# Order of the last group's second norm, gate and shared products, and GpSimd's ids in four steps

## The chip, the cores and the metric

One core of one Trainium2 chip. The time is device microseconds of one execution of the program. The engines are TensorE (PE), VectorE (DVE), ScalarE (ACT), GpSimd (POOL) and SyncE (SP); each works through its own instructions in their written order and waits on semaphores.

## The reference

A transformer layer on 16 images with 193 tokens each (a class token, 64 patches, 128 text tokens), 128 features wide:

```
h = concat(class, patches @ W + b) * pos;  h = concat(h, txt)
h = h + attention(layernorm(h))          # 8 heads, linear attention with elu + 1, rotary, a 3-tap convolution
x = layernorm(h)                         # the second norm
shared = (silu(x @ sw1) * (x @ sw3)) @ sw2
scores = x @ gate_w.T                    # 8 experts
idx = top_k(scores + biases, 2);  p = sigmoid(top_k(scores, 2)); p = p / sum(p)
h = h + shared + sum over the two experts e of a token:
        p_e * ((silu(x @ w1[e]) * (x @ w3[e])) @ w2[e])
```

## The kernel before

All is one core's work in three stages.

*Attention loop.* Two images make a group, so there are G = 8 groups of three 128-row tiles; the 16 class rows are one more tile (CLS), which goes with the last group. While group i is in the attention, the groups in front of it go through the second norm, the gate and the choice of experts. `choices(g)` (VectorE) finds both experts of each token, `place(g)` (TensorE) counts with matmuls how many tokens of an expert come before, `places(g)` and `positions(g)` (VectorE) make each token's row in the buffer `xs_dram`, and GpSimd scatters the normed rows there, two scatters a tile (L861). Each scattered row carries an id (where the result goes) and a share (its p). For groups 0 to 5 GpSimd makes both itself: `goals(g)` the ids, `shares(g)` the shares from ScalarE's exponentials (`odds`).

*Handover.* After the loop the last two groups finish these steps, while TensorE works through the shared products: for each chunk c of 384 tokens, `shared_up(c, m)` for m = 0, 1 (L1572, L1575, into two banks), `shared_silu(c, m)` (ScalarE, L675), `shared_mul(c, m)` (VectorE, L1159), `shared_down(c)` (TensorE, L1587), `shared_add(c)` (VectorE, L1165). A `shared_up` waits until the `shared_mul` two before it has read its bank. Chunks 0 to 5 and chunk 6's `shared_up` come ahead of the experts. ScalarE also rounds the eight experts' weights (`round_w13`, L614) and VectorE keeps what the rounding lost (`remainder_w13`, L1174). For the last group the chain is: second statistics and norm (`x2_done`), `turn_second` (L1477), ScalarE's copy of the turned rows (`x2T`, L723), `gate` (L1484), a copy of the scores, `choices`, `place`, `places`, `positions`, and GpSimd's last eight scatters. `turn_second(g)` also waits for `places(g - 1)`, which reads the same bank. ScalarE changes its function table between exp/ln and Silu (L695, L702, L713).

*Expert loop.* 56 tiles of 128 rows. SyncE loads them once all scatters have landed and the table of tiles is done; TensorE turns each (L1658), VectorE splits it (L1298, L1300), TensorE multiplies (L1669), and so on. Chunks 7 and 8 of the shared products follow behind.

The order on each engine is that of the code. Nothing else sets it.

## Time and profile before

| what | us |
|---|---|
| median of 3 runs | 250.85 (250.84 to 251.06) |
| the profiled execution's own time | 250.12 |
| its span, first to last instruction | 248.3 |
| TensorE busy | 221.4 (89%) |
| VectorE busy | 186.1 (75%) |
| ScalarE busy | 159.4 (64%) |
| GpSimd busy | 134.4 (54%) |

The attention loop ends at about 104 us, and the expert loop begins at about 147 us. A busy share is a mean over the stages; what ends a stage is read from the chain of waits and from the timeline of each engine. In a timeline a row is one instruction, or several of one kind that follow each other (x3), with the time when the first starts and the time until the last one's result; the next instruction of the engine can start a little before that.

### The profile page before, as it was taken

Reading aid. Unit: us, or ns where it says so; the run is one execution under the profiler, and the core shown is the slowest. Engines: PE = TensorE matmul, PEld = TensorE weight load, DVE = VectorE, ACT = ScalarE, POOL = GpSimd, SP = SyncE. Lnnn points to the kernel's source line nnn. Section 1 sums busy time; section 2 is a strip of 40 time slices with the busy share of each in tenths; the row PEclk is TensorE's granted clock in tenths of the full one; section 3 lists DMA queues with packets and bytes.
Section 4 is the critical chain, followed back from the end, with each engine's and each line's share of the span. In section 5 each row is a group of like instructions: output and inputs, shape, how many; then the busy total and the mean of one; then the engine's idle time right before and its main releaser. Section 6 shows DMA issues by size and latency. Waiting matters only on the chain.

```text
span 248.3 us, 5612 instructions
## 1 busy us (share of the span) xinstructions
PE 221.4 (89%) x1485; PEld 189.5 (76%) x1485; DVE 186.1 (75%) x706; ACT 159.4 (64%) x435; POOL 134.4 (54%) x178
## 2 busy tenths in 40 slices
PE   3898889999999999888989979999999999999930
PEld 2878778889898989756676658888888888887720
DVE  3548899998998989988977777666666666665760
ACT  3055676768687878869843266777777767776630
POOL 1400001258787778878777704666666666666500
PEclk9999999999999999999999999999999999999995
DMA  6999973142425101010113231423333333348657
GB/s 210 354 350 356 325 274 125 27 189 65 187 67 206 44 25 43 11 56 11 55 54 115 62 83 43 115 68 101 88 88 83 93 94 85 86 128 235 185 137 192
DMA packets 31566, 31.75 MB, mean 128 GB/s; under 512 B 4338, under 2 KB 27419, under 8 KB 30768
## 3 DMA queue, kind: packets, MB, share of 16 engines
q1 hardware_dynamic: 27240, 24.60, 32.7%
q0 software_dynamic: 3392, 6.38, 7.9%
q10 hardware_dynamic: 904, 0.41, 0.6%
q8 instruction: 13, 0.21, 0.4%
q14 instruction: 17, 0.14, 0.2%
HBM read 22.83 MB, written 9.06 MB: 128 GB/s over the span
## 4 chain that ended last, share of the span: by engine, by line
PE 57%; DVE 19%; issue 7%; ACT 6%; POOL 4%; DMA 4%; SPq 1%; DVEq 0%; POOLq 0%; ACTq 0%
PE bank L1669 15%; PE bank L1689 10%; PE bank L1678 5%; PE bank L1381 5%; POOL xs_dram L861 4%; DVE att L956 3%; DVE att L949 3%; DVE st L890 3%; PE bank L1658 3%; PE bank L1464 2%; PE bank L1450 2%; PE bank L1484 2%; DMA xp_both<-in_patches 2%; DVE hrow L998 2%; PE bank L1587 2%
## 5 line engine op out<-in xcount | busy, mean ns | idle before, releaser
L872 POOL DMA_INDIRECT y_dram<-att,goal x56 | 55.8, 996 | 35.8 <-ACT att L766 35.2
L861 POOL DMA_INDIRECT xs_dram<-xd,pos_i x50 | 52.2, 1044 | 21.8 <-issue 18.9
L1381 PE MATMUL bank<-wt,xp_both 128*128 128x128 f32 x288 | 40.7, 296 | 5.0 <-DMA xp_both<-in_patches 5.0
L1381 PEld LDWEIGHTS bank<-wt,xp_both 128*128 128x128 f32 x288 | 38.5, 208 | 6.3 <-DMA xp_both<-in_patches 5.3
L1689 PE MATMUL bank<-w_sb,att 128*128 x224 | 34.5, 277 | 0.0
L1298 DVE CAST xsT_h<-bank 128x128 fp32r<-128x128 f32 x56 | 16.3, 292 | 24.0 <-PE bank L1658 22.5
L752 ACT ACTIVATE att<-bank 128x256 f32<-128x256 f32 x56 | 21.5, 384 | 19.1 <-PE bank L1669 19.1
L1689 PEld LDWEIGHTS bank<-w_sb,att 128*128 128x128 f32 x224 | 29.4, 191 | 0.3 <-issue 0.2
L1669 PE MATMUL bank<-xp_both,xsT_h 128*128 x56 | 26.8, 479 | 0.0
L1311 DVE TENSOR_TENSOR att<-att,bank 128x256 f32<-128x256 f32 x56 | 23.2, 414 | 1.6 <-ACT att L752 1.6
L766 ACT ACTIVATE att<-bank,goal 128x128 f32<-128x128 f32 x56 | 20.6, 368 | 4.6 <-PE bank L1689 0.5
L1669 PE MATMUL bank<-xp_both,xsT_l 128*128 x56 | 22.1, 394 | 0.0
L1669 PE MATMUL bank<-w,xsT_h 128*128 x56 | 21.9, 392 | 0.0
L1678 PE MATMUL bank<-cst,att 128*128 128x128 f32 x112 | 21.5, 274 | 0.4 <-DVE att L1311 0.4
L759 ACT COPY att<-bank 128x256 f32<-128x256 f32 x56 | 20.9, 372 | 0.8 <-PE bank L1678 0.7
L1678 PEld LDWEIGHTS bank<-cst,att 128*128 128x128 f32 x112 | 13.8, 140 | 5.8 <-DVE att L1311 1.4
L1300 DVE TENSOR_TENSOR xsT_l<-bank,xsT_h 128x128 fp32r<-128x128 f32 x56 | 16.3, 292 | 1.9
L675 ACT ACTIVATE sh_s<-bank 128x384 f32<-128x384 f32 (+1 forms) x18 | 8.0, 456 | 13.3 <-PE bank L1575 12.4
L1658 PE MATMUL bank<-cst,xs_all 128*128 128x128 f32 x56 | 15.3, 273 | 1.4 <-DMA xs_all<-xs_dram 1.4
L1307 DVE COPY goal<-xs_all 128x2 f32<-128x2 f32 x56 | 14.9, 267 | 0.0
L1587 PEld LDWEIGHTS bank<-sw_sb,sh_h 128*128 128x128 f32 (+1 forms) x88 | 10.4, 187 | 5.2 <-DVE hrow L1165 2.2
L1572 PE MATMUL bank<-x2T,sw 128*128 128x384 f32 (+1 forms) x36 | 13.9, 467 | 0.4 <-DVE sh_h L1159 0.4
(225 smaller groups left out, 512.2 us busy)
## 6 DMA issues: line engine op xcount, KB each, us to landing
xp_both<-in_patches SPq DMA_DIRECT2D x6, 1152.0 KB
xs_all<-xs_dram SPq DMA_DIRECT2D x56, 65.0 KB, 1.9
xd<-y_dram SPq DMA_DIRECT2D x8, 384.0 KB, 5.1
w<-in_w SPq DMA_DIRECT2D x2, 1024.0 KB, 10.4
y_dram<-att,goal POOLq DMA_INDIRECT x56, 2.3
xs_dram<-xd,pos_i POOLq DMA_INDIRECT x50
xp_both<-in_patches SPq DMA_DIRECT2D x1, 768.0 KB, 5.4
hrow<-in_txt SPq DMA_DIRECT2D x2, 384.0 KB, 7.3
```

Of the source, the lines that this page charges most:

```text
L752: A(hs[q][:], bank[2 + q][:, 0:HID], ACT.Silu).then_inc(silu_done[at], 1)
L759: nc.scalar.copy(hmT[q][:], bank[4 + q][:, 0:HID].rearrange("p (m t) -> p m t", m=2)).then_inc(hmT_done[at], 1)
L766: A(ys[buf][:], bank[6 + q][:, 0:D], ACT.Copy, scale=goal[buf][:, 1:2]).then_inc(ys_done[at], 1)
L861: nc.gpsimd.indirect_dma_start(out=xs_dram[:, :], out_offset=bass.IndirectOffsetOnAxis(ap=pos_i[0:rows, j, k:k + 1], axis=0), in_=xd[0:row ...
L872: nc.gpsimd.indirect_dma_start(out=y_dram[:, :], out_offset=bass.IndirectOffsetOnAxis(ap=goal[u][:, 0:1].bitcast(I32), axis=0), in_=ys[u][ ...
L1298: V.tensor_copy(xsT_h[q][:], bank[q][:, 0:P]).then_inc(xh_done, 1)
L1311: V.tensor_tensor(hm[q][:], hs[q][:], bank[2 + q][:, HID:2 * HID], ALU.mult).then_inc(hm_done[at], 1)
L1381: M(ps[:, 0:D], xp[p][:, k, :], wt[:, k, :], start=(k == 0), stop=False)
L1658: T(bank[q][:, 0:P], xs[u][:, 0:D], ident).then_inc(tx_done[slot(u, 0)], 1)
L1669: last = M(bank[2 + q][:, 0:2 * HID], x[q][:], w[:, bass.ds(first * 2, 2 * HID)], start=(i == 0), stop=(i == 2))
L1678: last = T(bank[4 + q][:, P * m:P * m + P], hm[q][:, P * m:P * m + P], ident)
L1689: last = M(bank[6 + q][:, 0:D], hmT[q][:, m, :], w[:, bass.ds(first + m * D, D)], start=(m == 0), stop=(m == 1))
```

## The change

Four parts:

1. On VectorE, ScalarE and TensorE the last group's second norm, its rows and its gate stand ahead of shared products, and some weight remainders behind. 2. `s_col` and `scores(G - 2)` stand ahead of the Silu table on ScalarE. 3. GpSimd's `goals` makes both ids with one subtraction of six elements, one comparison and one addition (four instructions in place of five), from a second table in `dest_sb` that holds the bare row numbers. 4. The power in `shares` becomes a VectorE `RECIPROCAL` in `positions(g)`, g below 6: VectorE waits there for GpSimd's sum, GpSimd for the reciprocal.

```diff
-WEIGHED = 7
+WEIGHED = 6
+SUMMED = 5
...
@@ ScalarE, behind columns2(G - 2)
+            act.wait_ge(s_done, G)
+            nc.scalar.copy(s_col[:].rearrange("p (g b) -> p g b", b=2), s_all[:, :, 0:2]).then_inc(s_done, 1)
+            scores(G - 2)
             act.preload_act_table(ACT.Silu)
             shared_silu(0, 0)
-            scores(G - 2)
-            act.wait_ge(s_done, G)
-            nc.scalar.copy(s_col[:].rearrange("p (g b) -> p g b", b=2), s_all[:, :, 0:2]).then_inc(s_done, 1)
             shared_silu(0, 1)
-            round_w13(3)
             act.preload_act_table_set("natural_log_exp_and_others")
...
             act.preload_act_table(ACT.Silu)
             shared_silu(1, 0)
-            shared_silu(1, 1)
-            shared_silu(2, 0)
-            round_w13(4)
             act.wait_ge(nm2_done, G)
             A(xd[:, CLS - 1, 0, 0:D], hrow[:, CLS - 1, :], ACT.Identity, bias=nm2[:, CLS - 1:CLS],
               scale=rs2[:, CLS - 1:CLS]).then_inc(x2_done, 1)
+            shared_silu(1, 1)
+            shared_silu(2, 0)
+            round_w13(3)
             shared_silu(2, 1)
             act.wait_ge(x2_turned, G)
...
-            round_w13(5)
             act.wait_ge(gate_done, G)
...
+            round_w13(4)
+            shared_silu(3, 0)
+            round_w13(5)
+            shared_silu(3, 1)
             round_w13(6)
-            shared_silu(3, 0)
-            shared_silu(3, 1)
...
@@ GpSimd
-                then_pool(nc.gpsimd.tensor_tensor(crossed[:], chosen[:, :, 0], chosen[:, :, 1], ALU.subtract))
+                then_pool(nc.gpsimd.tensor_tensor(crossed[:], chosen[:], chosen[:, :, ::-1], ALU.subtract))
                 then_pool(nc.gpsimd.tensor_scalar(apart[:], crossed[:], 0.0, float(NID), ALU.is_gt, ALU.mult))
-                nc.gpsimd.tensor_tensor(xd[:, at, 0, D].bitcast(I32), ids[:, at, 0], apart[:], ALU.add)
-                nc.gpsimd.tensor_tensor(xd[:, at, 1, D].bitcast(I32), ids[:, at, 1], apart[:], ALU.subtract)
+                nc.gpsimd.tensor_tensor(xd[:, at, :, D].bitcast(I32), ids[:, at, :], apart[:], ALU.add)
...
-                then_pool(nc.gpsimd.tensor_tensor(odds_sum[:], odds_sum[:], minus[:], ALU.pow))
-                then_pool(nc.gpsimd.tensor_tensor(xd[:, at, :, D + 1], odds[:, :, ::-1], odds_sum[:].rearrange(
+                pool.wait_ge(pos_done, 2 * g + 1)
+                then_pool(nc.gpsimd.tensor_tensor(xd[:, at, :, D + 1], odds[:, :, ::-1], odds_part[:].rearrange(
...
-                pool.wait_ge(pos_done, g + 1)
+                pool.wait_ge(pos_done, g + 1 + min(g + 1, EARLIER))
@@ VectorE, positions(g)
+                if g < EARLIER:
+                    dve.wait_ge(pool_chain, WEIGHED * g + SUMMED)
+                    V.reciprocal(odds_part[:], odds_sum[:]).then_inc(pos_done, 1)
                 dve.wait_ge(pr_done, g + 1)
@@ VectorE, the handover (without its waits and its unchanged lines)
-            remainder_w13(0)
             places(G - 3)
             positions(G - 3)
+            remainder_w13(0)
...
-            remainder_w13(2)
             second_rows(G - 1)
-            shared_mul(0, 0)
             second_stats(G - 1)
...
-            shared_mul(0, 1)
+            shared_mul(0, 0)
...
+            shared_mul(0, 1)
             choices(G - 2)
-            shared_add(0)
-            shared_mul(1, 0)
...
-            shared_mul(1, 1)
-            places(G - 2)
-            positions(G - 2)
...
-            remainder_w13(3)
+            places(G - 2)
+            positions(G - 2)
+            shared_mul(1, 0)
+            shared_add(0)
+            shared_mul(1, 1)
+            remainder_w13(2)
+            choices(G - 1)
             shared_mul(2, 0)
-            shared_mul(2, 1)
-            remainder_w13(4)
-            shared_add(1)
-            choices(G - 1)
             places(G - 1)
             positions(G - 1)
...
+            shared_add(1)
+            shared_mul(2, 1)
+            remainder_w13(3)
+            shared_mul(3, 0)
             shared_add(2)
-            shared_mul(3, 0)
+            remainder_w13(4)
@@ TensorE, behind shared_up(2, 0)
             place(G - 2)
+            turn_second(G - 1)
             shared_up(2, 1)
+            gate(G - 1)
             shared_down(1)
-            turn_second(G - 1)
-            gate(G - 1)
-            shared_down(2)
             shared_up(3, 0)
             place(G - 1)
+            shared_down(2)
             shared_up(3, 1)
```

The instructions as they stand in both kernels, at three places. A line number of the kernel after is one or two off from that of the kernel before. First ScalarE from the copy of group 6's turned rows (`x2T`) on, before:

```order
L478 COPY x2T<-bank6 128x384
L695 ACT_TABLE_LOAD
L675 ACTIVATE sh_s0<-bank5 128x384
L488 COPY sc<-bank6 128x24
L699 COPY s_col<-s_all 128x16
L675 ACTIVATE sh_s1<-bank2 128x384
L614 CAST xp_both<-w13 128x512
L702 ACT_TABLE_LOAD
L707 ACTIVATE lv2<-mv2 128x3
L707 ACTIVATE lv2<-mv2 16x1
```

and after:

```order
L479 COPY x2T<-bank6 128x384
L697 COPY s_col<-s_all 128x16
L489 COPY sc<-bank6 128x24
L699 ACT_TABLE_LOAD
L676 ACTIVATE sh_s0<-bank5 128x384
L676 ACTIVATE sh_s1<-bank2 128x384
L702 ACT_TABLE_LOAD
L707 ACTIVATE lv2<-mv2 128x3
L707 ACTIVATE lv2<-mv2 16x1
```

The sum's class columns (`s_col`) and the scores (`sc`) have moved ahead of the table, and a rounding (L614) is gone from here.

TensorE from `shared_up(2, 1)` of the kernel before on (L1572 and L1575 are a `shared_up`, L1587 a `shared_down`, L1477 `turn_second`, L1484 the gate):

```order
L1572 MATMUL bank<-x2T,sw 128x384
L1575 MATMUL bank<-x2T,sw 128x384
L1587 MATMUL bank<-sw_sb,sh_h 128x128 x6
L1477 MATMUL bank<-cst,xd 128x128 x3
L1477 MATMUL bank<-cst,xd 128x16
L1484 MATMUL bank<-cols,x2T 128x8 x3
L1484 MATMUL bank<-cols,x2T 16x8
L1587 MATMUL bank<-sw_sb,sh_h 128x128 x6
L1572 MATMUL bank<-x2T,sw 128x384
L1575 MATMUL bank<-x2T,sw 128x384
```

and after, from `turn_second` on:

```order
L1479 MATMUL bank<-cst,xd 128x128 x3
L1479 MATMUL bank<-cst,xd 128x16
L1574 MATMUL bank<-x2T,sw 128x384
L1577 MATMUL bank<-x2T,sw 128x384
L1486 MATMUL bank<-cols,x2T 128x8 x3
L1486 MATMUL bank<-cols,x2T 16x8
L1589 MATMUL bank<-sw_sb,sh_h 128x128 x6
L1574 MATMUL bank<-x2T,sw 128x384
L1577 MATMUL bank<-x2T,sw 128x384
```

`turn_second` has moved ahead of `shared_up(2, 1)`, the gate behind it, and only one `shared_down` stands between the gate and `shared_up(3, 0)`. Behind `place(7)`, which ends with the total (L1501, now L1503), TensorE has before:

```order
L1498 MATMUL bank<-bc,ones_b 128x8
L1501 MATMUL bank<-total,ones_b 128x8
L1572 MATMUL bank<-x2T,sw 128x384
L1575 MATMUL bank<-x2T,sw 128x384
L1572 MATMUL bank<-x2T,sw 128x384
```

and after:

```order
L1500 MATMUL bank<-bc,ones_b 128x8
L1503 MATMUL bank<-total,ones_b 128x8
L1589 MATMUL bank<-sw_sb,sh_h 128x128 x6
L1574 MATMUL bank<-x2T,sw 128x384
L1577 MATMUL bank<-x2T,sw 128x384
L1574 MATMUL bank<-x2T,sw 128x384
```

The `shared_down` that stood behind the gate now stands here, ahead of `shared_up(3, 1)`.

VectorE up to the end of the last group's choices (L1034 writes `total`), before:

```order
L1159 TENSOR_TENSOR sh_h0<-sh_s0,bank1 128x384
L1159 TENSOR_TENSOR sh_h1<-sh_s1,bank0 128x384
L1174 TENSOR_TENSOR w13<-w13,xp_both 128x512
L1165 TENSOR_TENSOR hrow<-bank3,hrow 128x384
L1014 TENSOR_TENSOR scb<-sc,gateb_sb 128x32
L1017 MAX mx8<-scb 128x8 x4
L1022 MAX_INDEX ix8<-mx8,scb 128x8 x4
L1024 TENSOR_TENSOR pick<-cst,ix8 128x64
L1029 TENSOR_SCALAR pick<-pick,cst 128x16
L1030 TENSOR_TENSOR bc7<-pick 128x32
L1034 TENSOR_REDUCE total<-bc7 128x8
```

and after, from the end of these choices (L1033) on:

```order
L1029 TENSOR_TENSOR bc7<-pick 128x32
L1033 TENSOR_REDUCE total<-bc7 128x8
L1161 TENSOR_TENSOR sh_h0<-sh_s0,bank1 128x384
L1041 TENSOR_TENSOR prod<-pick,bank6 128x64
L1057 TENSOR_REDUCE pos_2<-prod 128x8
L1058 TENSOR_REDUCE pos_i<-pos_2 128x4
L1059 TENSOR_REDUCE pos_i<-pos_2 128x4
L1230 TENSOR_TENSOR tab_p<-bank6,cst 128x8
L1167 TENSOR_TENSOR hrow<-bank3,hrow 128x384
L1161 TENSOR_TENSOR sh_h1<-sh_s1,bank0 128x384
```

Before, both products of chunk 2 (L1159), a remainder (L1174) and `shared_add(1)` (L1165) stand ahead of the choices. After, the first product stands behind the choices, and the second behind places, positions (L1041 to L1059), `tab_p` and `shared_add(1)`.

## Rows read from the trace of the kernel before

**Rows 1.** Chain of waits, 100 to 150 us; columns: start us, us, what
```profile
123.25 0.65 PE bank L1575 x2
...
141.47 1.94 DMA xs_dram<-xd,pos_i
```

**Rows 2.** Timeline of TensorE, handover; columns: start us, us, instruction, [idle before <-releaser]
```profile
118.97 1.58 PE L1587 MATMUL bank<-sw_sb,sh_h 128*128 128x128 f32 x12
120.39 0.81 PE L1572 MATMUL bank<-x2T,sw 128*128 128x384 f32 x2
...
126.31 0.97 PE L1484 MATMUL bank<-cols,x2T 128*128 128x8 f32 x8 [0.58 <-ACT x2T L723]
...
130.40 0.89 PE L1572 MATMUL bank<-x2T,sw 128*128 128x384 f32 x2
...
146.75 0.49 PE L1669 MATMUL bank<-xp_both,xsT_h 128*128 x1
```

**Rows 3.** Timeline of VectorE, handover
```profile
116.25 0.56 DVE L998 TENSOR_TENSOR hrow<-bank,hrow 128x384 f32<-128x384 f32 x1
...
117.18 0.67 DVE L890 BATCH_NORM_STATS2 st<-hrow 128x6 f32<-128x128 f32 x3
...
118.12 0.25 DVE L1203 TENSOR_TENSOR hrow<-bank,hrow 16x128 f32<-16x128 f32 x1
...
122.81 0.18 DVE L1042 TENSOR_TENSOR prod<-pick,bank 128x48 f32<-128x48 f32 x1
...
123.41 0.84 DVE L1221 TENSOR_SCALAR xd<-hrow,rs,nm 128x128 f32<-128x128 f32 x3
...
127.57 0.19 DVE L1014 TENSOR_TENSOR scb<-sc,gateb_sb 128x32 f32<-128x32 f32 x1
...
129.72 0.22 DVE L1034 TENSOR_REDUCE total<-bc 128x8 bf16<-128x40 bf16 x1
130.58 0.22 DVE L1042 TENSOR_TENSOR prod<-pick,bank 128x64 f32<-128x64 f32 x1 [0.64 <-PE bank L1501]
...
146.24 0.29 DVE L1300 TENSOR_TENSOR xsT_l<-bank,xsT_h 128x128 fp32r<-128x128 f32 x1
```

**Rows 4.** Timeline of VectorE: positions in the attention loop, and a reciprocal
```profile
87.28 0.17 DVE L1052 TENSOR_REDUCE pos_i<-prod 128x6 int32<-128x48 f32 x1
...
99.41 0.17 DVE L1052 TENSOR_REDUCE pos_i<-prod 128x6 int32<-128x48 f32 x1
99.50 0.61 DVE L974 SCALAR_TENSOR_TENSOR hl<-xT,cols,hl 128x384 f32<-128x384 f32 x1
...
152.77 0.19 DVE L1287 RECIPROCAL mx<-mx 128x7 f32<-128x7 f32 x1
```

**Rows 5.** Timeline of TensorE: attend() in the attention loop
```profile
101.55 0.92 PE L1464 MATMUL bank<-qq,ksm 128*128 128x193 f32 x4 [0.24 <-ACT ksm L550]
```

**Rows 6.** Timeline of GpSimd: first scatters, ids and odds
```profile
51.66 1.25 POOL L861 DMA_INDIRECT xs_dram<-xd,pos_i  x1 [5.82 <-issue]
...
59.54 1.01 POOL L834 TENSOR_TENSOR crossed<-chosen 128x3 f32<-128x3 f32 x1
...
62.98 0.20 POOL L844 TENSOR_TENSOR odds_sum<-odds 128x3 f32<-128x3 f32 x1
...
86.75 0.19 POOL L834 TENSOR_TENSOR crossed<-chosen 128x3 f32<-128x3 f32 x1
...
88.60 0.38 POOL L844 TENSOR_TENSOR odds_sum<-odds 128x3 f32<-128x3 f32 x1
...
124.33 1.35 POOL L861 DMA_INDIRECT xs_dram<-xd,pos_i  x1 [0.30 <-issue]
```

**Rows 7.** Timeline of ScalarE, handover
```profile
114.79 1.28 ACT L695 ACT_TABLE_LOAD   x1
116.08 0.49 ACT L675 ACTIVATE sh_s<-bank 128x384 f32<-128x384 f32 x1
...
125.76 0.49 ACT L723 COPY x2T<-bank 128x400 f32<-128x400 f32 x1 [1.33 <-PE bank L1477]
```

More of the change, by code:

```diff
@@ L99, in destinations @@
     ids = flat + np.arange(2)[None, None, :] * NID
-    return np.concatenate([ids.reshape(P, 2 * J), np.full((P, 1), BIG)], 1).astype(np.int32)
+    flat = np.broadcast_to(flat, ids.shape)
+    return np.concatenate([ids.reshape(P, 2 * J), np.full((P, 1), BIG), flat.reshape(P, 2 * J)], 1).astype(np.int32)
 def build(nc, patches, txt, w_tok, cls, pos, wqk, bqk, small, gate_b,
@@ L122, in build @@
         ident, mask = cst[:, C_ID:C_ID + P], cst[:, C_MASK:C_MASK + P]
-        dest_sb = sb("dest_sb", [P, 2 * J + 1], I32)
+        dest_sb = sb("dest_sb", [P, 4 * J + 1], I32)
         wt = sb("wt", [P, KB, D])
@@ L190, in build @@
         pos_2 = sb("pos_2", [P, LATE, 2])
-        apart = sb("apart", [P, 3], I32)
+        apart = sb("apart", [P, 3, 2], I32)
         chosen = sb("chosen", [P, 3, 2])
-        crossed = sb("crossed", [P, 3])
+        crossed = sb("crossed", [P, 3, 2])
         odds = sb("odds", [P, 3, 2])
-        minus = sb("minus", [P, 3])
-        odds_sum = sb("odds_sum", [P, 3])
+        odds_sum, odds_part = sb("odds_sum", [P, 3]), sb("odds_part", [P, 3])
         pos_i = sb("pos_i", [P, J, 2], I32)
@@ L817, in _ @@
             nc.gpsimd.memset(xd[:, FROM:, :, D + 1:D + 2], 1.0).then_inc(ids_ready, 1)
-            nc.gpsimd.memset(minus[:], -1.0).then_inc(ids_ready, 1)
-            pool.wait_ge(ids_ready, 3)
-            ids = dest_sb[:, 0:2 * J].rearrange("p (j k) -> p j k", k=2)
+            pool.wait_ge(ids_ready, 2)
+            ids = dest_sb[:, 2 * J + 1:4 * J + 1].rearrange("p (j k) -> p j k", k=2)
             links = [0]
```

## The prediction

> **What bounds the kernel now.** I read three views in this order. The chain of waits first: up to 100 us it runs round the attention loop, from 147 us to the end round the expert loop on TensorE, and between them it ends in GpSimd's scatters, of which ten follow one another and the last lands at 141.47 + 1.94 = 143.41 [rows 1]. So at first sight the handover is bound by GpSimd. Then TensorE's own rows: in all that time it works through the shared products, and the first expert product starts at 146.75 [rows 2]. Then VectorE's: the last input that it makes for that product is ready at 146.24 + 0.29 = 146.53 [rows 3], only 0.22 us sooner, and in front of it stand the last shared products. So two lines arrive together: scatters, and shared products. Speeding one gives at most 0.22 us; delaying either costs nearly all of the delay, since the expert loop behind is a TensorE chain that gives nothing back.
>
> **The change part by part.** Times below are those of the profiled execution.
>
> *The loop.* positions(g) for g = 0 to 4 gets a RECIPROCAL. Three elements are not in the trace; seven take 0.19 [rows 4]. VectorE starts a small instruction some 0.09 after the last (99.41 to 99.50 [rows 4]), so each costs 0.09, or 0.19 if nothing overlaps. It delays nm1, ScalarE's rows and key sums behind it, and TensorE's attend(), which waits 0.24 for those sums and for nothing else [rows 5]. I find no cover: 5 x 0.09 = 0.45 us, with 0 to 0.95 as ends. positions(5) stands before a VectorE idle and costs nothing.
>
> VectorE now also waits there for GpSimd's odds_sum(g); queued behind it are tap_before, nm1 and heads, and TensorE waits for those. Six scatters and the step before them take 51.66 to 59.54 = 7.9 us; the steps from the subtraction to the odds' sum took 59.54 to 63.18 = 3.6 in group 1 and 86.75 to 88.98 = 2.2 in group 3 [rows 6], now one instruction fewer. Between VectorE's positions and the first scatter I allow 1.1 (group 6's first scatter at 124.33 comes 0.84 after its positions, and the share's product is ahead now [rows 3, 6]). Sum 11.0 to 12.6 against a loop of 99.41 - 87.28 = 12.13 [rows 4]. Mostly it fits; with four such groups (1 to 4) the ends are 0 and 4 x 0.5 = 2. I take 0.2, near the lower end, as the loop is the longer in most of that range.
>
> *GpSimd's four steps.* The id instruction and the power go. GpSimd reaches later groups sooner, but their scatters then wait for VectorE's positions, so nothing of it reaches the handover except through groups 6 and 7 (rivals).
>
> *ScalarE's table.* s_col and scores(6) now stand ahead of the Silu table. Before, the load ran from 114.79, in the idle of others, and the first Silu followed 0.01 behind it at 116.08 [rows 7]. Now ScalarE first waits for the attention's sum (VectorE's second rows start at 116.25, and mixed_rows and the sum come before; I put the sum at 115.6), copies twice, loads from 115.8 to 117.1 and has its first Silu done by 117.6.
>
> The page "ScalarE: Activation LUTs" of the Trainium skill (What ACT_TABLE_LOAD costs) adds a drain of 1380 ns to a load of 1283 ns at every switch of sets. The load agrees with 1.28; the 0.01 behind it [rows 7] shows no drain, and the measurement decides. By the page the first Silu would come 1.38 later, and the sum below would grow by about 1.
>
> *Norm and gate, forward.* The addition of second rows and the product behind it took 0.93 for two (116.25 to 117.18 [rows 3]), so 0.47 a piece and 0.55 to the result. Without a product between, the statistics wait for the addition's result, 116.25 + 0.56 = 116.8; the class row's addition follows 0.94 later (117.18 to 118.12 [rows 3]), at 117.75, and shared_mul(0,0) at 117.95, ready at 118.5. Before it was ready by 117.3, and here the loss starts: shared_up(1,1) takes its bank over and now waits until 118.5, a TensorE idle of 1.1.
>
> From there the chain is TensorE's. A shared_up takes 1.30 (two halves of 0.65 [rows 1], the last result 0.16 later), a shared_down 118.97 to 120.39 = 1.42 [rows 2]. shared_up(1,1) ends at 119.8, shared_down(0) at 121.2, shared_up(2,0) at 122.5, place(6) gives its result at 122.8. The second norm's rows are done long since, at 122.1: ahead of their 123.41 there stood two products, an addition and the 0.60 of places and positions [rows 3], 2.0 us in all. But turn_second(7) waits for places(6) too, and ScalarE's shared_silu(2,0) and TensorE's shared_up(2,1) wait for shared_mul(1,0), which VectorE now has behind positions(6): 122.8 + 0.60 = 123.4, ready at 124.0. shared_up(2,1) gives its result 1.46 later, at 125.45, and shared_silu(2,1) needs it. Behind that Silu, on ScalarE, stands the x2T copy of the last group: it takes 0.49 as before [rows 7], and is done at 126.4. The gate runs 126.4 to 127.4; it ran 126.31 to 127.28 [rows 2]. So the rows come 2 us sooner and the gate no sooner at all.
>
> *Behind the gate.* The scores' copy ends at 127.65. choices(7) takes 129.72 + 0.22 - 127.57 = 2.37 [rows 3] and ends at 130.0, place(7) at 130.4; VectorE's places(7) started at 130.58 before [rows 3], now at 130.45. Here the second and larger loss sits. Before, TensorE went from place(7) straight to shared_up(3,1) at 130.40 [rows 2]. Now shared_down(2) is there, and needs shared_mul(2,1), which VectorE does behind places, positions and tab_p (0.7, from the 0.60 for three tiles), shared_add(1) (0.47) and its own 0.55: ready at 132.2. TensorE idles 1.8 us, spends 1.42 on shared_down(2), and starts shared_up(3,1) at 133.65 in place of 130.40, 3.25 later. Everything behind it is the same in both kernels and in the same order, and was dense on TensorE; the weights' remainders that VectorE has put off fit into its idles there. So the last inputs come at 146.53 + 3.25 = 149.78 and the first expert product at 149.8: 3.05 later than 146.75.
>
> **Sum.** 250.12 + 3.05 + 0.45 + 0.2 = 253.82. The profiled execution lies 0.73 below the median of the runs (250.85), so 254.55 on that scale; I say 254.5.
>
> **Rivals.**
>
> *VectorE and GpSimd in lockstep.* The condition: GpSimd's steps fall beside VectorE's long rotary instructions in every group, not only in group 1. For it: the same subtraction took 1.01 us at 59.54 and 0.19 at 86.75 [rows 6], and since GpSimd is about 2 us sooner in each round, its steps move to where group 1's were. Against it: scatters then run free of them. Price: up to 0.5 more a round, 2 in all: 256.3. The page "SBUF — State Buffer" of the Trainium skill (Who interferes with whom) says that a VectorE instruction with two SBUF inputs holds off a GpSimd instruction that reads SBUF for its whole length. The 1.01 against 0.19 agrees.
>
> *The scatters alone bind (faster).* If the shared products had 3 us to spare, the end would go with GpSimd. positions(6) is ready at 123.5, GpSimd already waits and starts at 123.8, not 124.33 [rows 6]; the last group's positions at 131.2 are in time for a scatter line that ends 0.5 sooner. With the reciprocals hidden under the 0.24 [rows 5]: 250.85 - 0.5 = 250.3; with them on the path, 250.8, no change. It decides only if VectorE's first expert input comes by 146.6, which asks for shared_mul(2,1) 3 us sooner than I have it. The 0.22 of [rows 2, 3] speaks against it. The same case would be a gate that really comes forward: if ScalarE got to the x2T copy right behind turn_second(7), at 123.7, the gate would be at 125.4.
>
> *A part of the loss only.* The gate 1 us sooner than I put it and no loop cost: 250.85 + 2.0 = 252.9.
>
> **How the numbers follow.** A measurement of this kernel can tell about 0.2% (0.5 us) from no change. Forecast, 253.3 to 255.5: 0.68. Lockstep, 255.5 to 257.5: 0.12. Part of the loss, 251.4 to 253.3: 0.09. No change: 0.05. Faster: 0.06. So slower 0.89, same 0.05, faster 0.06. The range from 252.5 to 256.1 leaves out the two last cases and the outer halves of the others.
>
> **What would show it.** Right: TensorE idle of about 1 us ahead of the shared_up behind the class row, and of 1.8 ahead of the shared_down behind place(7), "released by VectorE's product"; the gate within 0.3 of 126.3 plus the loop's shift; GpSimd's last scatter long done when the first expert product starts; the expert loop and the tail unchanged in length. In the loop, RECIPROCAL rows below 0.2, and none of them with a wait on GpSimd longer than 0.3. Wrong: an x2T copy that starts at once behind turn_second(7), no idle behind place(7), or the chain of waits still in the scatters at 143 us.

## The result, and the profile after

| what | before | after |
|---|---|---|
| median in one comparison, us | 250.95 (250.84 to 251.36) | 256.33 (255.87 to 256.75) |
| the profiled execution's own time | 250.12 | 256.44 |
| its span | 248.3 | 254.4 |
| start of the attention's last sum (`s_all`) | 115.03 | 116.41 |
| start of the first expert product | 146.75 | 152.80 |
| the handover: from that sum to that product | 31.72 | 36.39 |
| from that product to the end of the span | 101.55 | 101.60 |

The changed kernel is slower, 1.022 times before (95% interval 1.0193 to 1.0247), some 5.4 us. The forecast had 3.6, and the median lies 0.2 us above its range. The profiled executions differ by 6.32 us: 1.38 arise in the attention loop, 4.67 in the handover, nothing in the expert loop (0.05), and the rest lies around the span. The ratios leave out executions more than 1.5% above the fastest of their kernel, of which there is one, e7's of 258.21 us.

**The loop.** VectorE's rows of groups 0, 3 and 4 (columns of a timeline as in [rows 2]) answer to [rows 4]:

```profile
50.41 0.17 DVE L1054 TENSOR_REDUCE pos_i<-prod 128x6 int32<-128x48 f32 x1
...
88.11 0.18 DVE L1050 RECIPROCAL odds_part<-odds_sum 128x3 f32<-128x3 f32 x1 [0.30 <-POOL odds_sum L843]
88.20 0.17 DVE L1054 TENSOR_REDUCE pos_i<-prod 128x6 int32<-128x48 f32 x1
...
100.70 0.17 DVE L1050 RECIPROCAL odds_part<-odds_sum 128x3 f32<-128x3 f32 x1 [0.30 <-POOL odds_sum L843]
100.79 0.17 DVE L1054 TENSOR_REDUCE pos_i<-prod 128x6 int32<-128x48 f32 x1
```

From one reduction to the next it is now 100.79 - 88.20 = 12.59 us, where it was 12.13. Over the four rounds from group 0 to group 4 it is 100.79 - 50.41 = 50.38, and before 99.41 - 50.54 = 48.87, by [rows 4] and this row:

```profile
50.54 0.17 DVE L1052 TENSOR_REDUCE pos_i<-prod 128x6 int32<-128x48 f32 x1
```

So the four rounds cost 1.51; the profile of after began them 0.13 sooner, which leaves the 1.38. The reciprocal itself shifts the reduction by 0.09; but it waits for GpSimd, 0.29 to 0.30 in each of groups 2 to 4. GpSimd's rows ahead of that wait, and VectorE's beside them:

```profile
84.30 0.95 POOL L833 CAST chosen<-ix 128x6 f32<-128x6 uint32 x1
85.33 0.80 POOL L834 TENSOR_TENSOR crossed<-chosen 128x6 f32<-128x6 f32 x1
86.22 0.97 POOL L835 TENSOR_SCALAR apart<-crossed 128x6 int32<-128x6 f32 x1
87.27 0.20 POOL L836 TENSOR_TENSOR xd<-dest_sb,apart 128x6 int32<-128x6 int32 x1
87.54 0.26 POOL L842 TENSOR_SCALAR odds<-odds 128x6 f32<-128x6 f32 x1
87.88 0.19 POOL L843 TENSOR_TENSOR odds_sum<-odds 128x3 f32<-128x3 f32 x1
88.43 0.53 POOL L845 TENSOR_TENSOR xd<-odds,odds_part 128x6 f32<-128x6 f32 x1 [0.35 <-DVE pos_i L1054]
...
96.88 0.96 POOL L833 CAST chosen<-ix 128x6 f32<-128x6 uint32 x1
...
100.47 0.19 POOL L843 TENSOR_TENSOR odds_sum<-odds 128x3 f32<-128x3 f32 x1
```
```profile
84.24 0.96 DVE L946 TENSOR_TENSOR att<-att,sinx 128x768 f32<-128x768 f32 x1
85.12 0.95 DVE L948 TENSOR_TENSOR att<-att,cosx 128x768 f32<-128x768 f32 x1
86.11 0.96 DVE L955 TENSOR_TENSOR att<-att 128x768 f32<-128x768 f32 x1
...
98.70 0.96 DVE L955 TENSOR_TENSOR att<-att 128x768 f32<-128x768 f32 x1
```

Each of GpSimd's first three steps ends within 0.12 us of a rotary instruction of VectorE, and takes 0.80 to 0.97 us; the fourth, with none beside it, 0.20. Before, group 3's subtraction ran behind the rotary instructions and took 0.19 [rows 6]. Added up, GpSimd's round is 0.32 from the reciprocal to the share's product (88.11 to 88.43), 8.45 for it and six scatters (to 96.88), 3.78 to the end of the next sum (100.66): 12.55, and 0.04 until the reciprocal. The chain of waits, which ran mostly over TensorE and VectorE in these rounds before, runs through GpSimd (columns as in [rows 1]):

```profile
83.33 0.96 POOL xs_dram L860
84.30 0.96 POOL chosen L833
```

But the round is also VectorE's own: from the reciprocal to its third rotary instruction 98.70 - 88.11 = 10.59, and from there 2.00 to the next reciprocal, the wait included. GpSimd's comparison ends with that rotary instruction (99.78 against 99.66), and the id, the odds and the sum behind it take 0.88 more, while VectorE's own work there takes 0.74. The sum is late by that difference in each round; e6 below tells the two readings apart.

**The handover on TensorE** (answers to [rows 2]):

```profile
119.93 0.91 PE L1574 MATMUL bank<-x2T,sw 128*128 128x384 f32 x2 [0.94 <-DVE sh_h L1161]
...
124.62 0.68 PE L1479 MATMUL bank<-cst,xd 128*128 128x128 f32 x4 [0.39 <-DVE prod L1041]
125.48 0.91 PE L1574 MATMUL bank<-x2T,sw 128*128 128x384 f32 x2 [0.18 <-DVE sh_h L1161]
...
128.00 0.97 PE L1486 MATMUL bank<-cols,x2T 128*128 128x8 f32 x8 [0.96 <-ACT x2T L723]
...
130.37 1.49 PE L1574 MATMUL bank<-x2T,sw 128*128 128x384 f32 x2
131.65 1.49 PE L1577 MATMUL bank<-x2T,sw 128*128 128x384 f32 x2
...
135.23 1.57 PE L1589 MATMUL bank<-sw_sb,sh_h 128*128 128x128 f32 x12 [1.92 <-DVE sh_h L1161]
136.64 0.81 PE L1574 MATMUL bank<-x2T,sw 128*128 128x384 f32 x2
...
152.80 0.49 PE L1671 MATMUL bank<-xp_both,xsT_h 128*128 x1 [0.75 <-DVE xsT_l L1302]
```

All four idle stretches of the forecast are there: 0.94 before shared_up(1,1), 0.39 and 0.18 at turn_second(7) and shared_up(2,1), 0.96 before the gate, 1.92 before shared_down(2). shared_up(3,1) starts at 136.64, 6.24 later than the 130.40 of [rows 2]. New is shared_up(3,0): the pair takes 2.56 us (130.37 to 132.93) where another takes 1.30. The windows say why (columns: window, its length, then busy us and instructions of PE, PEld, DVE, ACT and POOL, granted clock, DMA share, GB/s):

```profile
126.00:130.00 4.00, 3.04 (x21) 2.24 (x20) 1.62 (x9) 2.38 (x11) 3.09 (x4) 1.00 0.15 50
130.00:132.00 2.00, 2.00 (x8) 1.39 (x7) 1.86 (x12) 0.55 (x2) 1.39 (x3) 0.58 0.10 33
132.00:134.00 2.00, 1.31 (x9) 0.44 (x7) 0.67 (x5) 0.82 (x2) 0.83 (x1) 0.57 0.21 67
134.00:136.00 2.00, 0.77 (x7) 0.80 (x8) 1.68 (x6) 0.17 (x1) 1.33 (x2) 1.00 0.09 27
```

TensorE's granted clock was near 0.5, the 1.2 GHz level, for most of 130 to 134 us; it was 1.00, the 2.4 GHz level, before and behind, and all through the handover in the profile of before. The fall stands ahead of the 1.92 us of idle here, and behind the 0.96 before the gate.

**ScalarE** (answers to [rows 7]): its table load waits for the attention's sum, and the copy of the turned rows (L723) stands right behind a Silu that waited for TensorE.

```profile
117.01 0.20 ACT L697 COPY s_col<-s_all 128x16 f32<-128x16 f32 x1 [0.86 <-DVE s_all L991]
...
117.31 1.28 ACT L699 ACT_TABLE_LOAD   x1
118.61 0.87 ACT L676 ACTIVATE sh_s<-bank 128x384 f32<-128x384 f32 x2
...
127.07 0.49 ACT L676 ACTIVATE sh_s<-bank 128x384 f32<-128x384 f32 x1 [0.56 <-PE bank L1577]
127.46 0.49 ACT L723 COPY x2T<-bank 128x400 f32<-128x400 f32 x1
```

### The profile page after: what moved, and what is told of

Its sections match the earlier page's. It is cut to its first block, busy times and chain, and to the rows that moved or that the text cites. A ratio compares the mean times of both kernels' runs of the same rounds, so it can differ in the third digit from the quotient of the medians.

```text
span 254.4 us, 5603 instructions
## 1 busy us (share of the span) xinstructions
PE 221.5 (87%) x1477; PEld 188.9 (74%) x1485; DVE 186.5 (73%) x712; ACT 159.0 (62%) x435; POOL 130.6 (51%) x165
## 4 chain that ended last, share of the span: by engine, by line
PE 52%; DVE 17%; POOL 12%; issue 7%; ACT 5%; SPq 3%; DMA 2%; DVEq 0%; POOLq 0%
PE bank L1671 15%; PE bank L1691 10%; POOL xs_dram L860 7%; PE bank L1680 5%; PE bank L1589 4%; PE bank L1574 3%; PE bank L1577 3%; PE bank L1660 2%; DMA xp_both<-in_patches 2%; DVE att L955 2%; DVE st L889 2%; DVE att L948 2%; DVE sh_h L1161 1%; PE bank L1486 1%; POOL apart L835 1%
## 5 line engine op out<-in xcount | busy, mean ns | idle before, releaser
L860 POOL DMA_INDIRECT xs_dram<-xd,pos_i x50 | 50.4, 1009 | 18.5 <-issue 12.8
L1383 PE MATMUL bank<-wt,xp_both 128*128 128x128 f32 x288 | 39.6, 291 | 6.6 <-DMA xp_both<-in_patches 6.6
L1383 PEld LDWEIGHTS bank<-wt,xp_both 128*128 128x128 f32 x288 | 37.5, 203 | 8.0 <-DMA xp_both<-in_patches 5.5
L1574 PE MATMUL bank<-x2T,sw 128*128 128x384 f32 (+1 forms) x36 | 14.6, 488 | 1.2 <-DVE sh_h L1161 1.1
L1589 PE MATMUL bank<-sw_sb,sh_h 128*128 128x128 f32 (+1 forms) x88 | 11.6, 280 | 4.2 <-DVE sh_h L1161 2.4
```

What stands on the lines that cost most here:

```text
L860: nc.gpsimd.indirect_dma_start(out=xs_dram[:, :], out_offset=bass.IndirectOffsetOnAxis(ap=pos_i[0:rows, j, k:k + 1], axis=0), in_=xd[0:row ...
L1383: M(ps[:, 0:D], xp[p][:, k, :], wt[:, k, :], start=(k == 0), stop=False)
L1574: M(bank[second][:, 0:n], sw13[:, HID + P * m:HID + P * m + P], x, start=True, stop=True)
L1589: last = M(bank[3][0:rows, D * t:D * t + D], hidden_of(c, m)[:, P * t:P * t + rows], sw2_sb[:, m, :], start=(m == 0), stop=(m == 1))
```

## The experiments

Each was timed beside before on its chip; the ratio is to that. "Handover" is the stretch of the table above, in the run's profile. My theory after the traces: order 3.1 us, loop 1.5, clock 1.3. The rivals stand with each run; in the first four texts the theories are called A, B and C.

| run | median us | before | ratio, 95% interval | handover us |
|---|---|---|---|---|
| e1 | 254.66 | 250.85 | 1.015 (1.011 to 1.0191) | 36.68 |
| e2 | 251.57 | 250.85 | 1.0044 (1.0014 to 1.0075) | 31.67 |
| e3 | 250.76 | 250.85 | 1.0002 (0.9979 to 1.0025) | 31.67 |
| e4 | 254.95 | 250.85 | 1.0175 (1.0139 to 1.021) | 34.88 |
| e5 | 256.69 | 251.14 | 1.0219 (1.0179 to 1.0258) | 35.08 |
| e6 | 251.35 | 251.14 | 1.0006 (0.998 to 1.0032) | 31.65 |
| e7 | 254.27 | 251.14 | 1.012 (1.0077 to 1.0162) | 33.83 |
| e8 | 257.30 | 251.14 | 1.0246 (1.0205 to 1.0287) | 35.59 |
| e9 (after) | 256.27 | 250.46 | 1.0231 (1.019 to 1.0271) | 36.74 |
| e10 | 253.34 | 250.46 | 1.0118 (1.0085 to 1.0152) | 33.63 |
| e11 | 251.56 | 250.46 | 1.0039 (1.0011 to 1.0067) | 32.03 |
| e12 | 255.31 | 250.74 | 1.02 (1.0159 to 1.0241) | 35.07 |
| e13 | 254.31 | 250.74 | 1.0136 (1.0098 to 1.0175) | 33.76 |
| e14 | 252.45 | 250.82 | 1.0068 (1.0041 to 1.0095) | 32.73 |

**e1: parts 1 and 2 alone** (the order of VectorE, ScalarE and TensorE, as in the change's diff; GpSimd as before).

> The change's order on ScalarE, VectorE and TensorE, with GpSimd's ids, power and waits as before and no reciprocal. Theory A (three losses that add up: 1.5 us in the attention loop because VectorE now waits for GpSimd, 3.1 us in the handover's order, 1.3 us because TensorE's clock falls once in the handover): the attention's last sum on VectorE starts at 115.0 as before, the first expert product at 149.8 if the clock holds and at 151.1 if it falls; 254.0 to 255.4 us, slower than before by 3.1 to 4.4. Rival B (the wait on GpSimd costs little, the order costs all 5.4): 256 us. Rival C (the order costs little, most is GpSimd's line): under 252.5 us.

Measured: 1.5% slower. The loop's four rounds are as before (98.36 - 49.49 = 48.87). The last sum at 115.06 is before's only by chance: this profile began the rounds 1.05 sooner and lost it to a fall of the clock between 100 and 116 us. The idle stretches are those of after (0.93, 0.39, 0.96, 1.92), and the clock falls behind the last of them, from 134 us on (0.50). The order, with that fall, carries most of the loss, as theory A has it.

**e2: parts 3 and 4 alone** (ids in four steps, reciprocal on VectorE, both waits; the order as before).

> The change's GpSimd part alone (four id steps, the reciprocal on VectorE, the waits both ways), with the order of before. Theory A: the loop's period grows from 12.13 to 12.60, the attention's last sum starts 1.4 us later (116.4), the handover is as before: 252.3 us. Rival B: at most 0.5 us slower, 251.4. Rival C: 254 us or more.

Measured: the last sum at 116.33, the handover as before, 31.67. From group 0 to the last sum it takes 65.99, before 64.49: the loop's 1.50 are all in these two parts. So theory A by the trace; the median lies between A (252.3) and B (251.4), up by 0.4% (0.1 to 0.8%). The clock hides part of the loss in it: eleven of e2's twelve executions have a mean granted clock of 0.987 or more, and only nine of the 23 of before beside it have 0.984 or more. These eleven take 251.57 on average, those nine 250.13, which is 1.4. e1 and e2 add up to 1.9%, against 2.2% for both.

**e3: four id steps, the power left on GpSimd.**

```diff
 before, and
+                then_pool(nc.gpsimd.tensor_tensor(crossed[:], chosen[:], chosen[:, :, ::-1], ALU.subtract))
...
+                nc.gpsimd.tensor_tensor(xd[:, at, :, D].bitcast(I32), ids[:, at, :], apart[:], ALU.add)
```

> The kernel before with the four id steps, but the power left on GpSimd, so that VectorE waits for nothing of GpSimd's in the loop. Theory A: the loop's period is 12.13 as before, GpSimd is ahead of the kernel before by 0.3 to 0.6 us a group, its scatters of group 6 then wait for positions and start 0.3 to 0.5 us sooner, and the shared products allow 0.2 of that: 250.7 us, no change that can be measured. Rival (each GpSimd instruction saved shortens the handover one for one): 249.0 us.

Measured: no change (1.0002), theory A. Behind the attention's last sum the tile loads come 1.05 us sooner (141.96 - 114.39 = 27.57, before 143.65 - 115.03 = 28.62), and TensorE no longer waits for them, but the handover, 31.67, is what it was. So the four steps cost nothing; part 4 does. And speeding the scatters alone gives nothing, as the forecast had it of its two lines [rows 2, 3].

**e4: shared_up(3,1) ahead of shared_down(2) in after.**

```diff
             place(G - 1)
-            shared_down(2)
             shared_up(3, 1)
+            shared_down(2)
```

> The changed kernel with shared_down(2) put back behind shared_up(3, 1) on TensorE, nothing else. Theory A: TensorE starts shared_up(3, 1) directly behind place(7) and shared_down(2) finds its product ready, so the idle of 1.9 us and the shared_down in front of it go; the shared line ends 1.9 us sooner (the shared_down itself is still to be done), 254.4 us. If the idle comes back at the next wait for VectorE: 256 us.

Measured: the 1.92 us go, and waits of 0.23 and 1.05 for VectorE's products come up behind. The handover is 1.5 shorter than after's, of which 1.3 is the clock (1.00 in the handover), as e12 shows: the move itself is worth 0.2. The median lies between the two expectations.

**e5: idle stretches filled, the early ones.**

```diff
             mixed_cls()
+            pe.wait_ge(sc_done, G - 1)
+            fill(bank[6], (384, 128))
             shared_up(1, 1)
...
             shared_up(2, 1)
+            pe.wait_ge(sh_mul, 4)
+            fill(bank[5], (384, 128))
             gate(G - 1)
```

> The changed kernel; TensorE does throw-away products (384 and 128 columns, into banks that are free) in two of its idle stretches: before shared_up(1,1), where it waited 0.94 us, and before the last gate, where it waited 0.96 us. They take about 0.87 us each, less than the waits, so no useful instruction has to start later. Theory clock (the idle stretches make the granted clock fall to 0.58 between 130 and 134 us, and that costs the 1.27 us by which shared_up(3,0) was longer): granted clock 1.00 there, shared_up(3,0) 1.30 us, shared_down(2) at 134.0 in place of 135.23, total about 255.0. Rival (the fall has another cause, or what it takes is given back by the wait behind place(7)): the clock falls as before, or it doesn't fall and the total stays at 256.0 to 256.6.

Measured: in the profile the clock is 1.00 from 126 to 140 us, shared_up(3,0) takes 1.3 and the handover is 35.08, 1.3 less than after's. But the median is no better than after's, and four of its six executions had a mean granted clock of 0.980 or less, as three of after's four do: filling these two, with the 1.92 still there, is not enough.

**e6: the reciprocal without the wait for GpSimd.** It leaves the odds' sum out of the shares.

```diff
-                    dve.wait_ge(pool_chain, WEIGHED * g + SUMMED)
-                    V.reciprocal(odds_part[:], odds_sum[:]).then_inc(pos_done, 1)
+                    V.reciprocal(odds_part[:, g, :], cst[:, C_ONES:C_ONES + 3]).then_inc(pos_done, 1)
```

> Before's order with the four id steps, where VectorE's RECIPROCAL stays in its place and size but reads a table of ones, and its result is kept in six buffers: VectorE waits for GpSimd no more. It leaves the odds' sum out of the shares. GpSimd's own work stays as it is. Theory lockstep (it is the wait for GpSimd's sum that sets the loop's period to 12.60): the period is back at 12.13 to 12.22, the attention's last sum at 115.0 to 115.5 in place of 116.33, and the total 250.9 to 251.3. Rival (the RECIPROCAL itself, or what it does to VectorE's later instructions, makes the loop longer): period 12.4 to 12.6, the last sum at 116, total 251.6 or more.

Measured: no slower than before, and its rows give 100.07 - 87.88 = 12.19 us a round. The last sum comes at 115.69, later than expected, but this profile began the rounds 0.43 later than before's.

```profile
87.82 0.14 DVE L1049 RECIPROCAL odds_part<-cst 128x3 f32<-128x3 f32 x1
87.88 0.17 DVE L1053 TENSOR_REDUCE pos_i<-prod 128x6 int32<-128x48 f32 x1
...
100.01 0.14 DVE L1049 RECIPROCAL odds_part<-cst 128x3 f32<-128x3 f32 x1
100.07 0.17 DVE L1053 TENSOR_REDUCE pos_i<-prod 128x6 int32<-128x48 f32 x1
```

The instruction is worth 0.06 a round, the wait 0.4: the wait is what makes the loop longer. It is not the length of GpSimd's round that does it. Without the wait GpSimd's steps meet the same rotary instructions and take the same time (0.94, 0.79 and 0.97 in group 4), its round is 100.17 - 87.97 = 12.20, as long as VectorE's, and still its sum ends 0.36 behind VectorE's reciprocal (100.37 against 100.01):

```profile
98.51 0.97 POOL L835 TENSOR_SCALAR apart<-crossed 128x6 int32<-128x6 f32 x1
...
100.17 0.20 POOL L843 TENSOR_TENSOR odds_sum<-odds 128x3 f32<-128x3 f32 x1
```
```profile
98.39 0.96 DVE L955 TENSOR_TENSOR att<-att 128x768 f32<-128x768 f32 x1
```

From the reciprocal to that rotary instruction VectorE takes 98.39 - 87.82 = 10.57, as in after (10.59); from there to the reciprocal 1.62, in after 2.00.

**e7: the copy of the turned rows ahead of two Silus in after.**

```diff
             shared_silu(1, 1)
+            act.wait_ge(x2_turned, G)
+            nc.scalar.copy(x2T[:, 3 * P * (G - 1):3 * P * (G - 1) + 3 * P + B], bank[6][:, 0:3 * P + B]).then_inc(x2T_done, 1)
             shared_silu(2, 0)
             round_w13(3)
             shared_silu(2, 1)
```

> The changed kernel; ScalarE copies the last group's turned rows (x2T) ahead of shared_silu(2,0) and shared_silu(2,1) and not behind them. Theory (the gate came no sooner because that copy stood behind shared_silu(2,1)): the copy starts at about 125.4 in place of 127.46, the gate runs right behind shared_up(2,1) at 126.9 to 127.0 in place of 128.00, and all behind it comes 1.0 us sooner, with the clock as it is: 255.3; if the clock stays at 1.00 as well, 254.0. Rival (the wait is only handed on): the gate is 1 us sooner, but the idle before shared_down(2) grows by as much, and the total stays at 256.0 to 256.6.

Measured: the copy at 125.31, the gate right behind shared_up(2,1), 1.15 sooner, and all behind it moves along; the 1.92 stay as they were:

```profile
126.85 0.87 PE L1486 MATMUL bank<-cols,x2T 128*128 128x8 f32 x8
...
132.66 1.58 PE L1589 MATMUL bank<-sw_sb,sh_h 128*128 128x128 f32 x12 [1.92 <-DVE sh_h L1161]
```

So the Silu ahead of the copy is what kept the gate late, as the forecast said. The handover, 33.83, is 1.24 below e5's and e12's.

**e8: products ahead of the choices in after.**

```diff
+            shared_mul(2, 0)
+            shared_mul(2, 1)
             choices(G - 1)
-            shared_mul(2, 0)
+            shared_add(1)
             places(G - 1)
...
-            shared_add(1)
-            shared_mul(2, 1)
```

> The changed kernel; on VectorE shared_mul(2,0) and shared_mul(2,1) stand ahead of choices(7), and shared_add(1) ahead of places(7). Theory (the 1.92 us of TensorE's idle behind place(7) are the price of VectorE's order, and VectorE stood idle for 2.31 us ahead of choices(7)): shared_down(2) follows place(7) at once, choices(7) starts no later, the first expert product comes 1.4 to 1.9 sooner, total 254.4 to 254.9. Rival (GpSimd's scatters bind by then): TensorE's idle is gone, but the first expert product waits for the tile's DMA, and less than 1 us is gained: 255.4 or more.

Measured: neither theory; it is slower than after by its handover without a fall of the clock (35.59 against 35.07). I had overlooked that shared_mul(2,0) writes the buffer that shared_down(1) reads, and shared_down(1) stands behind the gate now. So VectorE waits for TensorE, with the choices queued behind:

```profile
130.82 1.02 DVE L1161 TENSOR_TENSOR sh_h<-sh_s,bank 128x384 f32<-128x384 f32 x2 [3.66 <-PE bank L1589]
131.76 0.18 DVE L1013 TENSOR_TENSOR scb<-sc,gateb_sb 128x32 f32<-128x32 f32 x1
```

With the gate ahead of shared_down(1), the order on VectorE behind it is hardly free.

**e9: after once more, and e12: its long idle stretch filled.**

```diff
             place(G - 1)
+            pe.wait_ge(sh_mul, 5)
+            for n in (384, 384, 256):
+                M(bank[2][:, 0:n], sw13[:, 0:P], x2T[:, 0:n], start=True, stop=True)
             shared_down(2)
```

> The changed kernel as it is, once more, beside the two below on one chip, for the clock. Theory (idle stretches in its handover make the granted clock fall, and this kernel pays for it more often than the one before): its mean clock lies below 0.984 in clearly more of its runs than in runs of before (about half to two thirds so far), and its runs at 0.986 or more take 255.0 to 255.4. Rival (falls come to every kernel alike): the same share of runs, and the median is 255.5 to 256.5 with runs at 0.986 or more close to it.

> The changed kernel; TensorE does throw-away products (384, 384 and 256 columns, into a bank that is free by then) in the one long idle stretch that is left untouched so far: between place(7) and shared_down(2), where it waited 1.92 us. They take about 1.73 us, less than the wait. Theory (this idle stretch is what the clock answers to): granted clock 1.00 from 126 to 140 us in the profile, mean clock 0.984 or more in all or nearly all runs as in the two kernels without it (e4 and e10: 12 of 12; e9: 1 of 6), median 255.0 to 255.4. Rival (the falls come from elsewhere): runs at 0.98 or less as often as before, median 256 to 256.6.

Measured: e9 repeats the result (1.0231); its mean granted clock was 0.980 or less in five of six executions. In its profile the clock falls again, right behind the 1.92 of idle, and the first two products there take 2.54 and 1.49 in place of 1.58 and 0.81:

```profile
133.36 2.54 PE L1589 MATMUL bank<-sw_sb,sh_h 128*128 128x128 f32 x12 [1.92 <-DVE sh_h L1161]
135.69 1.49 PE L1574 MATMUL bank<-x2T,sw 128*128 128x384 f32 x2
```
```profile
134.00:136.00 2.00, 2.00 (x10) 2.00 (x10) 0.00 (x0) 0.00 (x0) 1.69 (x2) 0.50 0.66 195
```

In e12 TensorE multiplies for nothing in that stretch, the mean clock is 0.989 or more in five of six executions, and the profile has 1.00 all through the handover:

```profile
131.60 1.99 PE L1630 MATMUL bank<-x2T,sw 128*128 128x384 f32 x6
133.42 1.54 PE L1589 MATMUL bank<-sw_sb,sh_h 128*128 128x128 f32 x12
```

The median is 255.31, in the theory's bounds, and the handover 1.3 to 1.7 shorter than after's and e9's with the same useful work. Its ratio, 1.02, and e9's have intervals that overlap, so the times alone do not settle it. With the clocks, and with e4 and e10, which have no such stretch and a mean of 0.984 or more in all twelve executions, they speak for this: in e9's place the idle stretch brings the fall about, not in every execution, and a fall in the handover costs 1.3 to 1.7 us. For the fall of after's own profile it is not shown: that one began at about 130.3, ahead of the 1.92 of idle and 2.3 us behind the 0.96 before the gate, which e12 leaves as it is. Nor is shown what makes the clock fall elsewhere: before's executions beside these runs had a mean of 0.983 or less in 42 of 79 (251.34 us on average, the other 37 took 250.26), and e1, e11 and e13 show falls between 100 and 116 us too.

**e10: e7 and e4 together; e13: and VectorE's first products back; e14: and ScalarE's table back.**

```diff
 e13, against e10, on VectorE
             second_rows(G - 1)
+            shared_mul(0, 0)
             second_stats(G - 1)
...
-            shared_mul(0, 0)
+            shared_mul(0, 1)
             dve.wait_ge(h2_done, G + 1)
...
 e14, against e13, on ScalarE
-            act.wait_ge(s_done, G)
-            nc.scalar.copy(s_col[:].rearrange("p (g b) -> p g b", b=2), s_all[:, :, 0:2]).then_inc(s_done, 1)
-            scores(G - 2)
             act.preload_act_table(ACT.Silu)
             shared_silu(0, 0)
+            scores(G - 2)
+            act.wait_ge(s_done, G)
+            nc.scalar.copy(s_col[:].rearrange("p (g b) -> p g b", b=2), s_all[:, :, 0:2]).then_inc(s_done, 1)
```

> The changed kernel with two edits together: ScalarE's copy of the last group's turned rows (x2T) ahead of shared_silu(2,0) and (2,1), and TensorE's shared_up(3,1) ahead of shared_down(2). Theory (they mend different waits: the gate behind the Silu, 1.0 us, and the idle behind place(7), of which 0.6 to 0.7 is left as a gain when the next wait has come up): the first expert product at 149.6, total 253.4 to 253.8 with the clock at 1.00 in the handover. Rival (both draw on the same slack): no better than with the copy alone, 150.2 and 254.3.

> The kernel of e10, and VectorE's shared_mul(0,0) and shared_mul(0,1) back at their old places, ahead of second_stats(7) and of the class row's statistics. Theory (the 0.94 us that TensorE waited before shared_up(1,1) are most of what is left of the handover's loss): that wait is gone, and the first expert product comes 0.6 to 0.9 sooner than in e10 (149.65, its last sum at 116.02), total 252.4 to 252.8. Rival (the wait is handed on to turn_second(7) and shared_up(2,1), which waited 0.39 and 0.19): less than 0.3 is gained.

> The kernel of e13, and ScalarE's Silu table and shared_silu(0,0) back ahead of scores(6) and s_col. Theory (the wait before shared_up(1,1) came from ScalarE: shared_silu(0,0) stood behind s_col, which waits for the attention's sum, and a table load of 1.28 us): TensorE no longer waits before shared_up(1,1), and the first expert product comes 33.0 us or less behind the attention's last sum (33.76 in e13, 31.72 before); total 252.6 to 253.0. Rival (the chain of VectorE, which makes the choices of group 6 and the last rows ahead of the products, sets turn_second(7) and shared_up(2,1), and takes the gain back): 33.4 or more, total 253.2 or more.

Measured: e10's times are those of the theory (253.34, first expert product at 149.65), but 0.4 of that is a last sum that came sooner than e7's, and beside its own before it is no better than e7 (1.0118 and 1.012). Its handover, 33.63, is 0.2 below e7's, the same 0.2 as between e4 and e12. That is nearer to the rival. e13 gains nothing, but not for the rival's reason: shared_up(1,1) still waits 0.74, and VectorE's product ahead of it waits for ScalarE:

```profile
120.55 0.55 DVE L1161 TENSOR_TENSOR sh_h<-sh_s,bank 128x384 f32<-128x384 f32 x1 [0.94 <-ACT sh_s L676]
```
```profile
121.16 0.91 PE L1574 MATMUL bank<-x2T,sw 128*128 128x384 f32 x2 [0.74 <-DVE sh_h L1161]
```

e14 takes that wait away and is 1.03 better, 32.73 (115.99 to 148.72).

So the first of the four stretches is ScalarE's: shared_silu(0,0) stands behind `s_col`, which waits for the attention's sum, and behind a table load.

**e11: shared products brought forward, with e3's ids.** Its edits, among them

```diff
             choices(G - 2)
-            shared_add(0)
             shared_mul(1, 0)
...
+            shared_mul(1, 1)
+            shared_add(0)
             dve.wait_ge(nm2_done, G)
```

> Before's kernel with the four id steps (power on GpSimd, no wait of VectorE), and a handover that brings the shared products forward in place of the norm: on VectorE shared_mul(1,0) and positions(6) stand ahead of shared_add(0), shared_mul(1,1) behind them, additions and remainders later; on ScalarE shared_silu(1,0) ahead of the ln table, rounding later; on TensorE turn_second(7) behind shared_up(2,1), gate(7) behind shared_down(1), shared_down(2) behind shared_up(3,0), later shared_downs one shared_up later. Theory (with the scatters sooner by the id steps, VectorE's and TensorE's shared line sets the end): TensorE is dense, the first expert product comes 1.0 to 1.6 us sooner than before's 146.75, total 249.3 to 250.0. Rival (another wait takes over, GpSimd's scatters or the tile's DMA): 250.5 to 251.

Measured: the rival, and somewhat worse than it (251.56, 1.0039). The shared line got shorter, but turn_second(7) waits 1.08 for rows that VectorE makes later, and the first tile's load comes later, with 1.48 of waiting:

```profile
125.11 0.71 PE L1477 MATMUL bank<-cst,xd 128*128 128x128 f32 x4 [1.08 <-DVE xd L1221]
...
146.61 0.33 PE L1658 MATMUL bank<-cst,xs_all 128*128 128x128 f32 x1 [1.48 <-DMA xs_all<-xs_dram]
```

No version was found that is faster than before.

## Why the prediction was wrong in size

Its sum was 253.82 for the profiled execution, and 256.44 came. Of the 2.62 us, the clock is 1.32 (after's handover less e12's), the loop 0.73 (0.86 by its rounds, less the 0.13 of the earlier start), the handover's order 0.30, and 0.27 lie in the tail and around the span. On the medians, 256.33 against 254.5, the clock is less: before pays for falls too, 1.1 us in 42 of 79 executions, and after in eight of ten (its own four and e9's six). My estimate from these counts is 0.8 x 1.3 - 0.53 x 1.1, some 0.5. There the loop is the larger error.

- **The step that failed: "Mostly it fits ... I take 0.2, near the lower end".** The wait costs 1.28 in place of 0.2: the four rounds are 1.51 longer, and only 0.23 of it is the instruction (in e6, with the instruction and without the wait, they take 100.07 - 50.97 = 49.10, against 48.87). Nearly all comes in the last three rounds, 0.4 in each. The step compared the length of GpSimd's round with the loop's, and charged only what the one exceeds the other by. That is not what the wait costs. GpSimd's three steps end with VectorE's rotary instructions, with the wait and without it; three more steps follow, and the sum ends 0.36 behind the point where VectorE needs it, even where GpSimd's round fits into the loop's (12.20 beside 12.19, e6). The step's low end rested on [rows 6] of group 3, where GpSimd's subtraction ran behind the rotary instructions; with the id instruction and the power gone it comes 1.4 sooner there (85.33 against 86.75).
- This was the first rival, at a chance of 0.12, and its condition came true word for word, for the reason it gave. Its price of 2 did not (1.28), and that its 256.3 is the measured median is luck: it held no clock. The sign that the forecast named, no wait on GpSimd longer than 0.3, could not tell: the waits are 0.29 to 0.30. The instruction costs 0.06 a round (e6), in place of the 0.09 taken.
- The page "SBUF — State Buffer" of the Trainium skill (Who interferes with whom) has it that a VectorE instruction with two SBUF inputs holds a GpSimd instruction that reads SBUF off for its whole length. The rows agree: 0.80 to 0.97 beside such instructions, 0.20 without.
- **A term that was missing: the clock.** The forecast put a 1.8 us idle stretch on TensorE and took it to cost its own length; a fall of the granted clock stood nowhere in it. In the profiles of after and e9 one cost 1.3 and 1.7 us more in the handover. e12 speaks for the idle stretch as the cause in e9; in after's profile the fall came ahead of it, and its cause stays open.
- **The handover's order, 3.05, was right:** 3.35 without the clock (e12 and e5). The gate "no sooner at all", behind the Silu: right (128.00 less the loop's 1.38 is 126.62, against 126.31; e7). The stall behind place(7), 1.8: right (1.92), but less a loss of its own than said. Moving shared_down(2) away gives 0.2 at the full clock (e4 against e12; e10 against e7), since shared_down(3) then waits 1.05, and e7 takes 1.24 off the handover with the 1.92 left as they were.
- **"Here the loss starts", with shared_mul(0,0) behind the class row:** right in place and size (1.1 forecast, 0.94 measured), wrong in cause. With the product back at its old place 0.74 of the wait are left, and it is ScalarE's late table that holds it (e13, e14). The forecast had worked that out too (first Silu done by 117.6; it was 119.1, the attention's sum being later) but compared it with nothing.
- The page "ScalarE: Activation LUTs" of the Trainium skill (What ACT_TABLE_LOAD costs) has a drain of 1380 ns behind a load. Again none is seen: the Silu starts 0.02 behind the load's end (117.31 + 1.28 = 118.59, then 118.61).
- GpSimd's four steps alone: no gain, as said (e3). The expert loop unchanged: as said.
- About 1.0 of the 3.35 is left in e14, with the waits of 0.39, 0.19 and 1.05 still there; which edit makes them was not tried.

## What to carry to other kernels

A wait of one engine for another is not priced by comparing the lengths of their rounds. Ask at which moment of the round the value is needed, and at which it is there: here the rounds were level at 12.2 us, and the value came 0.36 late in each. Where an earlier copy or table load stands on an engine that feeds a bank of the busiest one, look for what it pushes back before looking at what it brings forward. An idle stretch of TensorE can cost more than its length, when the clock falls behind it, as in e9. And a median over executions with and without such falls can hide a loss that the rows of a trace show (e2).

## What the hardware showed that was not expected

- Behind 1.92 us of idle, TensorE's granted clock fell to 0.50 (e9, 134 to 136 us), and a shared_down took 2.54 in place of 1.58. With useless products in that stretch the mean clock was 0.989 or more in five of six executions, where it had been 0.980 or less in five of six, and the median 255.31 in place of 256.27 (on two chips; beside their own before 1.020 and 1.0231, with intervals that overlap). In the profiles of e5 and e7 the same stretch is there without a fall.
- A tiny GpSimd instruction (128x6 elements) takes 0.20 or 0.97 us, by what VectorE does beside it, and a chain of three of them follows VectorE's instructions end for end (within 0.12).
